# A kernel of four blocks on one core: the state-space stage's skip term as a diagonal product on TensorE, its input scaled by ScalarE, other orders of waits and steps

## The chip, the cores and the metric

One core of one Trainium2 chip runs the whole program. The metric is the time of one execution on the device in microseconds, as the median of several. The engines of the core are TensorE (PE in the profile, with its weight loads as PEld), VectorE (DVE), ScalarE (ACT), GpSimd (POOL) and SyncE (SP), which only issues transfers. Each works through its own list of instructions and waits on semaphores for the others.

## What is computed

The input is 16 sequences of 256 positions with 128 features, in float32. Four blocks follow each other, each fed with the layer norm of the running sum and added to it: a state-space block, a block of local attention and a gated product (two layers), a power-attention block, and the second one again. Only the first is touched. Cut to what matters:

```python
x    = resid * lax.rsqrt(jnp.mean(resid * resid, -1, keepdims=True) + EPS) * norm_w
skip = x @ skip_w.T
xe   = x @ in_w.T                       # 256 channels, then a causal convolution of 4 taps
xs   = silu(conv(xe) + conv_b)
delta = softplus(xs @ wd1.T @ wd2.T + wd2_b)
Bm, Cm = xs @ wb.T, xs @ wc.T           # 16 states
h    = exp(d_l * A) * h + (d_l * x_l) * b_l      # over the 256 positions
y_l  = sum over states of h * c_l
y    = y + xs * W_D                     # the skip term of the change
y    = (y * silu(skip)) @ out_w.T
return resid + y
```

## The kernel before

The 256 channels lie as two blocks (c) of 128 partitions, positions along the free axis. One sequence is a unit of work. Its 16 states are done in 8 groups g of 2, so a group is a tile of 128 x (2 states x 2 blocks x 256 positions) = 128 x 1024. The steps are named in four tables, and the number in a name is the group:

- TensorE: xT transposes the scaled input, xe is the input projection with the convolution folded in (8 matmuls), skip the gate's projection, u and z the two matmuls of delta, bc those of Bm and Cm, bB and bC broadcast one group's rows of Bm and Cm over the partitions, y adds up m_hc of a group into bank[1] by a product with the identity, out is the output projection.
- ScalarE: sq squares for the norm, xTe copies xT out with the weight of the norm, xs and gate are the SiLUs, abs, exp and ln belong to softplus, hi, mid and mid2 split Bm and Cm in bfloat16 parts, a is exp(delta A) of a group (4 instructions), c copies the broadcast Cm.
- VectorE: xr scales the input, ue copies u, r1 and lo are the rest of the split, delta ends softplus, bx is the product of a group into PSUM (L502), h its scan (L509), ys adds xs W_D to y (L514), yg multiplies with the gate (L519), x adds the output to the stream (L523).
- GpSimd: me and rr (the norm's root), dx, xx, and hc, the scan's result times c (two instructions, L547).

M_STAGES gives each step a stage 0, 1 or 2, and M_ORDER gives each engine's list. run_windows goes through an engine's list once per window k, and a step of stage n works on sequence k - n; so three sequences are under way at a time, and the engines' windows needn't coincide. The order is thus written out by hand. Every step signals one semaphore count; `m_before(s, i, step, g, back)` is the wait for the step that used the same buffer `back` groups ago. m_h and m_c have two buffers, m_hc four, and bank[1] holds y and then the output projection. Between the dependent engines the key lines are:

```python
pe.wait_ge(*dve_m.at(i, "lo"))                        # bB, bC
dve.wait_ge(*pe_m.at(i, f"bB{g}"))                    # bx
act.wait_ge(*m_before(dve_m, i, "h", g, 2))           # a
pool.wait_ge(*dve_m.at(i, f"h{g}"))                   # hc
```

## Time and profile before

| | |
|---|---|
| median of 3 runs | 3156.47 us (3153.13 to 3156.8) |
| profiled execution | 3154.61 us, span 3152.8 us |
| state-space stage | from about 31 to 597.6 us of the span |
| busy in the whole span | TensorE 86%, VectorE 78%, ScalarE 72%, GpSimd 43% |
| mean granted clock of TensorE | 0.954 |

The span goes from the first to the last instruction. Shares of busy time over the whole span mix stages with different limits; what the stage of the change is bound by is read in stretches within it. A timeline row gives the start, the busy time from the first to the last of the merged instructions, the engine, the line, the operation with its tiles, and in brackets the idle time before it with what ended it.

### The profile page before, as it was taken

The page shows a single profiled execution, that of the slowest core. Times are in us where ns is not written, and L with a number is a line of the kernel's source. Part 1 is how long each engine was busy: PE and PEld are TensorE (multiplying, and loading weights), DVE is VectorE, ACT ScalarE, POOL GpSimd, SP SyncE. Part 2 cuts the span into 40 slices and gives each one's busy share as a digit, 9 for nine tenths or more (in the row PEclk, how much of TensorE's full clock was granted, in tenths as well). Part 3 has the DMA queues.
Part 4 walks back from the last instruction along what each step waited for, and adds up shares of the span by engine and source line. Part 5 has one row for each costly group of instructions (what it writes and reads, how often), then busy time and mean ns, then how long its engine had stood idle before and what let it go on. Part 6 is the DMA issues. An engine that isn't in the chain of part 4 may idle for free. (4 is left out here: it accounts for less than half of the span.)

```text
span 3152.8 us, 55672 instructions
## 1 busy us (share of the span) xinstructions
PE 2699.7 (86%) x18784; PEld 1825.4 (58%) x18784; DVE 2472.1 (78%) x3831; ACT 2254.9 (72%) x5987; POOL 1352.2 (43%) x1073
## 2 busy tenths in 40 slices
PE   4888888579999999999669999995799999999996
PEld 2444444246666666666447777774566666666664
DVE  6999999767777777777468888887677777777773
ACT  4888888357767677677459999994577766777673
POOL 4666666535545455454310000001445544455452
PEclk9999999789999999999879999997899999999997
DMA  3000000000000000000000000000000000000000
GB/s 88 1 1 1 1 1 1 1 1 2 1 1 1 12 12 1 2 1 1 23 1 2 2 1 2 1 2 1 1 1 1 1 1 12 12 1 1 1 1 27
DMA packets 17237, 17.75 MB, mean 6 GB/s; under 512 B 3997, under 2 KB 14942, under 8 KB 16862
## 3 DMA queue, kind: packets, MB, share of 16 engines
q1 hardware_dynamic: 16958, 14.19, 1.5%
q8 instruction: 155, 2.54, 0.3%
q14 instruction: 124, 1.02, 0.1%
HBM read 12.09 MB, written 2.10 MB: 5 GB/s over the span
## 5 line engine op out<-in xcount | busy, mean ns | idle before, releaser
L906 POOL TENSOR_TENSOR f_p<-f_p,f_rs 128x512 f32<-128x512 f32 (+1 forms) x256 | 320.9, 1253 | 735.9 <-DVE f_rs L855 735.9
L751 ACT ACTIVATE f_p<-pair,f_nm 128x128 f32<-128x128 f32 (+1 forms) x1024 | 389.0, 392 | 192.5 <-DVE f_nm L844 191.7
L898 POOL TENSOR_TENSOR f_qb<-f_kn,f_tab 128x512 f32<-128x512 f32 x256 | 444.2, 1756 | 173.5 <-DVE f_kn L824 173.5
L547 POOL TENSOR_TENSOR m_hc<-m_h,m_c 128x512 f32<-128x512 f32 x256 | 328.5, 1304 | 170.9 <-DVE m_h L509 169.7
L509 DVE TENSOR_TENSOR_SCAN m_h<-m_a,pair 128x1024 f32<-128x1024 f32 x128 | 292.1, 2282 | 2.9
L705 PE MATMUL bank<-f_hnT,f_w 128*128 128x256 f32 (+1 forms) x768 | 214.0, 402 | 80.9 <-DVE f_u L881 77.7
L623 PE MATMUL pair<-f_wqkv,f_hT 128*128 128x512 f32 x512 | 256.9, 625 | 9.8 <-DVE f_kn L824 7.9
L814 DVE TENSOR_REDUCE f_ss<-f_sq 128x16 f32<-128x1024 f32 x128 | 155.2, 1212 | 139.5 <-ACT f_sq L722 139.5
L407 PE MATMUL bank<-m_hc,ident 128*128 128x512 f32 x512 | 258.5, 651 | 4.7 <-POOL m_hc L547 4.7
L666 PE MATMUL pair<-ident,f_p 128*128 128x128 f32 x1536 | 245.8, 283 | 16.6 <-POOL f_p L906 6.9
L1160 POOL TENSOR_TENSOR X<-X,p_y 128x256 f32<-128x256 f32 x16 | 11.7, 730 | 567.6 <-DVE p_y L1154 567.6
L830 DVE TENSOR_TENSOR f_qa<-f_kn,f_tab 128x1024 f32<-128x1024 f32 x128 | 240.3, 1877 | 0.2
L465 ACT ACTIVATE m_a<-m_delta,m_A 128x255 f32<-128x255 f32 x512 | 216.0, 495 | 25.1 <-DVE m_h L509 24.0
L680 PEld LDWEIGHTS pair<-f_pT,f_v 128*64 128x64 f32 x3072 | 149.7, 136 | 141.6 <-issue 139.0
L844 DVE TENSOR_REDUCE f_nm<-pair 128x4 f32<-128x512 f32 (+1 forms) x256 | 208.6, 815 | 12.2 <-PE pair L653 10.1
L837 DVE TENSOR_TENSOR f_qa<-f_qa,f_qb 128x1024 f32<-128x1024 f32 x128 | 185.1, 1446 | 41.0 <-POOL f_qb L898 41.0
L653 PE MATMUL pair<-f_kT,f_qT 64*128 64x128 f32 (+1 forms) x2048 | 212.9, 327 | 0.0
L751 ACT ACTIVATION_READ_ACCUMULATOR f_p<-pair,f_nm 128x1 f32 x1024 | 207.8, 203 | 0.0
L705 PEld LDWEIGHTS bank<-f_hnT,f_w 128*128 128x128 f32 (+1 forms) x768 | 123.7, 181 | 139.5 <-DVE f_u L881 106.4
L638 PE MATMUL bank<-ident,f_qa 128*128 128x128 f32 x1024 | 162.8, 282 | 48.2 <-DVE f_qa L837 40.7
L680 PE MATMUL pair<-f_pT,f_v 128*64 128x128 f32 (+1 forms) x3072 | 197.9, 264 | 5.8 <-DVE f_pT L849 4.0
L666 PEld LDWEIGHTS pair<-ident,f_p 128*128 128x128 f32 x1536 | 169.1, 142 | 57.0 <-POOL f_p L906 33.2
(181 smaller groups left out, 6563.5 us busy)
## 6 DMA issues: line engine op xcount, KB each, us to landing
f_wqkv<-in_f_wqkv SPq DMA_DIRECT2D x4, 768.0 KB, 4.0
X<-in_x SPq DMA_DIRECT2D x16, 128.0 KB, 2.6
out_x<-X SPq DMA_DIRECT2D x16, 128.0 KB, 2.0
f_w<-in_f_w SPq DMA_DIRECT2D x4, 341.0 KB, 3.4
f_wo<-in_f_wo SPq DMA_DIRECT2D x4, 256.0 KB, 2.7
sel<-in_sel SPq DMA_DIRECT2D x1, 768.0 KB
f_w<-in_f_w SPq DMA_DIRECT2D x4, 192.0 KB, 3.2
p_wqk<-in_p_wqk SPq DMA_DIRECT2D x1, 512.0 KB
```

The lines of the kernel that those rows point to most:

```text
L407: mm = nc.tensor.matmul(bank[1][:], ident[:], m_hc[:, g % 4, n].rearrange("p c l -> p (c l)"), start=g == 0 and n == 0, stop=g == NG - 1 a ...
L465: op = nc.scalar.activation(m_a[:, g % 2, n, c, 1:L], m_delta[:, b, c, 1:L], ACT.Exp, scale=m_A[:, c, g * GN + n:g * GN + n + 1])
L509: op = nc.vector.tensor_tensor_scan(m_h[:, g % 2].rearrange(flat), m_a[:, g % 2].rearrange(flat), pair[2][:], 0.0, ALU.mult, ALU.add)
L547: op = nc.gpsimd.tensor_tensor(m_hc[:, g % 4, n], m_h[:, g % 2, n], m_c[:, g % 2, n].unsqueeze(1).broadcast_to([P, EC, L]), ALU.mult)
L623: mm = nc.tensor.matmul(half(pair[0], n), f_hT[:, t * P:t * P + P], fw["wqkv"][:, n * 512:n * 512 + 512], start=True, stop=True)
L666: mm = nc.tensor.transpose(PT_PS[:, j * P:j * P + P], f_p[:, t, j, y * P:y * P + P], ident[:])
L680: mm = nc.tensor.matmul(OT_F[DH * e:DH * e + DH, c, q0:q1], f_v[:, b, y, h, :], w, start=y == 1 or t == 0, stop=y == 0, skip_group_check=True)
L705: mm = nc.tensor.matmul(bank[1][0:HR[c], n * L:n * L + L], fw["w1"][:, x * HID + c * P:x * HID + c * P + HR[c]], f_hnT[:], start=True, sto ...
L751: op = nc.scalar.activation(f_p[:, t, j, k0:k1], SC[:, j, k0:k1], ACT.Exp, bias=f_nm[:, t, j:j + 1], accum_out=f_sm[:, t, j:j + 1])
L830: op = nc.vector.tensor_tensor(f_qa[:, t].rearrange("p (x h) d -> p x h d", x=2), f_kn[:, t].rearrange("p (x h) d -> p x h d", x=2), f_tab ...
L898: op = nc.gpsimd.tensor_tensor(f_qb[:, t, :, o].rearrange("p (x h) d -> p x h d", x=2), f_kn[:, t, :, 32 - 32 * e:64 - 32 * e].rearrange(" ...
L906: op = nc.gpsimd.tensor_tensor(f_p[:, t, :, k0:k1], f_p[:, t, :, k0:k1], f_rs[:, t, :].unsqueeze(2).broadcast_to([P, 4, k1 - k0]), ALU.mult)
```

## The change

The skip term leaves VectorE: the tile m_skip holds, for each block, the identity times W_D, made once before the stage, and after the last y step two matmuls of 256 columns add m_skip times m_xs into the same PSUM bank. ys and its tile m_y are gone, and yg reads the bank itself. The scaling xr goes to ScalarE, as a copy with a scale for each partition; the constant factor (the root of 128) moves into m_nw, the norm's weight used in xTe. The waits of y, xTe, c, bx, h and hc stand in another order, the one for the producer last. xs now waits for yg of two sequences ago, as ys is gone. M_STAGES and M_ORDER are new for all four engines (their core is shown).

```diff
 M_ORDER = {
-    "dve": "bx5 h5 r1 bx6 delta h6 lo bx7 xr h7 bx0 h0 bx1 ys h1 yg bx2 h2 x bx3 h3 ue bx4 h4",
-    "pe": "bC7 y4 y5 bB0 bC0 xT bB1 bC1 y6 y7 xe bB2 bC2 out skip bB3 bC3 u bC4 bB4 y0 y1 bB5 z bB6 bC5 bc bC6 y2 y3 "
-        "bB7",
-    "act": "a0 xTe c0 a1 sq c1 a2 xs c2 a3 c3 a4 gate a5 c4 abs c5 exp hi a6 ln mid2 c6 c7 mid a7",
-    "pool": "hc0 hc1 hc2 me hc3 rr hc4 hc5 dx hc6 xx hc7"}
+    "dve": "bx1 h1 bx2 yg h2 bx3 h3 ue bx4 x h4 bx5 h5 r1 bx6 delta h6 lo bx7 h7 bx0 h0",
+    "pe": "bB7 bB0 y4 bB1 bC0 y5 y6 bC1 y7 bB2 xT bC2 bB3 xe bC3 skip bB4 u bB5 out bc bC4 z bC5 y0 bB6 y1 bC6 y2 y3 "
+        "bC7",
+    "act": "xTe sq c2 a3 xs c3 gate a4 c4 a5 abs c5 exp hi ln a6 mid2 a7 c6 mid a0 c7 a1 c0 xr a2 c1",
+    "pool": "dx hc6 xx hc7 me rr hc0 hc1 hc2 hc3 hc4 hc5"}
...
-        m_y = m_sb("m_y", [P, EC, L])
+        m_skip = m_sb("m_skip", [P, EC, P])
+        m_nw = m_sb("m_nw", [P, 1])
...
-                pe.wait_ge(*dve_m.at(i, "xr"))
+                pe.wait_ge(*act_m.at(i, "xr"))
...
             elif k == "y":
-                pe.wait_ge(*pool_m.at(i, f"hc{g}"))
                 if g == 0:
                     pe.wait_ge(*dve_m.at(i - 1, "x"))
+                pe.wait_ge(*pool_m.at(i, f"hc{g}"))
                 for n in range(GN):
                     mm = nc.tensor.matmul(bank[1][:], ident[:], m_hc[:, g % 4, n].rearrange("p c l -> p (c l)"),
-                                          start=g == 0 and n == 0, stop=g == NG - 1 and n == GN - 1)
+                                          start=g == 0 and n == 0, stop=False, skip_group_check=True)
+                if g == NG - 1:
+                    for c in range(EC):
+                        mm = nc.tensor.matmul(m_y_ps[:, c, :], m_skip[:, c, :], m_xs[:, b, c, :], start=False,
+                                              stop=c == EC - 1, skip_group_check=True)
...
+            elif s == "xr":
+                act.wait_ge(*pe_m.at(i - 1, "xT"))
+                act.wait_ge(*pool_m.at(i, "rr"))
+                for t in range(T):
+                    op = nc.scalar.activation(m_xr[:, t, :], tiles(seq(Z, z_at))[:, t, :], ACT.Copy, scale=m_rr[:, t:t + 1])
             elif s == "xTe":
+                act.wait_ge(const_set, 17)
+                act.wait_ge(*pe_m.at(i - 1, "skip"))
                 act.wait_ge(*pe_m.at(i, "xT"))
-                act.wait_ge(*pe_m.at(i - 1, "skip"))
-                op = nc.scalar.activation(m_xT[:, CONV - 1:], m_xT_ps, ACT.Copy, scale=mw["norm_w"][:])
+                op = nc.scalar.activation(m_xT[:, CONV - 1:], m_xT_ps, ACT.Copy, scale=m_nw[:])
...
             elif s == "xs":
                 act.wait_ge(*pe_m.at(i, "xe"))
-                act.wait_ge(*dve_m.at(i - 2, "ys"))
+                act.wait_ge(*dve_m.at(i - 2, "yg"))
                 for c in range(EC):
...
             elif k == "c":
+                act.wait_ge(*m_before(pool_m, i, "hc", g, 2))
                 act.wait_ge(*pe_m.at(i, f"bC{g}"))
-                act.wait_ge(*m_before(pool_m, i, "hc", g, 2))
...
-            if s == "xr":
-                dve.wait_ge(*pool_m.at(i, "rr"))
-                dve.wait_ge(*pe_m.at(i - 1, "xT"))
-                for t in range(T):
-                    op = nc.vector.tensor_scalar(m_xr[:, t, :], tiles(seq(Z, z_at))[:, t, :], m_rr[:, t:t + 1],
-                                                 float(D) ** 0.5, ALU.mult, ALU.mult)
-            elif s == "ue":
...
             elif k == "bx":
+                dve.wait_ge(*pool_m.at(i, "dx"))
                 dve.wait_ge(*pe_m.at(i, f"bB{g}"))
-                dve.wait_ge(*pool_m.at(i, "dx"))
                 dve.wait_ge(*m_before(dve_m, i, "h", g, 1))
...
             elif k == "h":
+                dve.wait_ge(*m_before(pool_m, i, "hc", g, 2))
+                dve.wait_ge(*act_m.at(i, f"a{g}"))
                 dve.wait_ge(*dve_m.at(i, f"bx{g}"))
-                dve.wait_ge(*act_m.at(i, f"a{g}"))
-                dve.wait_ge(*m_before(pool_m, i, "hc", g, 2))
...
-            elif s == "ys":
+            elif s == "yg":
+                dve.wait_ge(*pe_m.at(i - 1, "out"))
                 dve.wait_ge(*pe_m.at(i, f"y{M_LAST}"))
-                for c in range(EC):
-                    op = nc.vector.scalar_tensor_tensor(out=m_y[:, c, :], in0=m_xs[:, b, c, :], scalar=mw["W_D"][:, c:c + 1],
-                                                        in1=m_y_ps[:, c, :], op0=ALU.mult, op1=ALU.add)
-            elif s == "yg":
-                dve.wait_ge(*dve_m.at(i, "ys"))
-                dve.wait_ge(*pe_m.at(i - 1, "out"))
-                op = nc.vector.tensor_tensor(m_yg[:], m_y[:], m_gate[:, b], ALU.mult)
+                op = nc.vector.tensor_tensor(m_yg[:], m_y_ps, m_gate[:, b], ALU.mult)
...
             elif k == "hc":
+                pool.wait_ge(*m_before(pe_m, i, "y", g, 4))
+                pool.wait_ge(*act_m.at(i, f"c{g}"))
                 pool.wait_ge(*dve_m.at(i, f"h{g}"))
-                pool.wait_ge(*act_m.at(i, f"c{g}"))
-                pool.wait_ge(*m_before(pe_m, i, "y", g, 4))
...
+            nc.vector.tensor_scalar(m_nw[:], mw["norm_w"][:], float(D) ** 0.5, None, ALU.mult).then_inc(const_set, 1)
+            for c in range(EC):
+                op = nc.vector.tensor_scalar(m_skip[:, c, :], ident[:], mw["W_D"][:, c:c + 1], None, ALU.mult)
+            op.then_inc(const_set, 1)
```

What stands in a row on VectorE, before, from a product with ys behind it to the scan after ue (pair<- is the product bx, m_h the scan h):

```order
L502 TENSOR_TENSOR pair<-m_dx,pair 128x1024
L514 SCALAR_TENSOR_TENSOR m_y<-m_xs,m_W_D,bank 128x256 x2
L509 SCALAR_TENSOR_TENSOR m_h<-m_a,pair 128x1024
L519 TENSOR_TENSOR m_yg<-m_y,m_gate 128x512
L502 TENSOR_TENSOR pair<-m_dx,pair 128x1024
L509 SCALAR_TENSOR_TENSOR m_h<-m_a,pair 128x1024
L523 TENSOR_TENSOR X<-m_xx,bank 128x256
L502 TENSOR_TENSOR pair<-m_dx,pair 128x1024
L509 SCALAR_TENSOR_TENSOR m_h<-m_a,pair 128x1024
L484 COPY m_u<-bank 64x256
L502 TENSOR_TENSOR pair<-m_dx,pair 128x1024
L509 SCALAR_TENSOR_TENSOR m_h<-m_a,pair 128x1024
```

ys, yg, x and ue follow each other at one group's distance. VectorE at the same place after the change (lines are those of the new kernel: L506 the product, L513 the scan):

```order
L506 TENSOR_TENSOR pair<-m_dx,pair 128x1024
L518 TENSOR_TENSOR m_yg<-bank,m_gate 128x512
L513 SCALAR_TENSOR_TENSOR m_h<-m_a,pair 128x1024
L506 TENSOR_TENSOR pair<-m_dx,pair 128x1024
L513 SCALAR_TENSOR_TENSOR m_h<-m_a,pair 128x1024
L488 COPY m_u<-bank 64x256
L506 TENSOR_TENSOR pair<-m_dx,pair 128x1024
L522 TENSOR_TENSOR X<-m_xx,bank 128x256
L513 SCALAR_TENSOR_TENSOR m_h<-m_a,pair 128x1024
```

ys is gone, and yg and x now stand between a product and its scan; ue stands before x. r1, delta and lo keep their places; xr is gone from behind the product bx7.

ScalarE before, from xs (L437) over the exponentials a (L465) and the copies c (L470) to the gate (L431):

```order
L437 ACT_TABLE_LOAD
L437 ACTIVATE m_xs<-pair,m_conv_b 128x256 x2
L470 ACTIVATE m_c<-pair 128x512
L465 ACT_TABLE_LOAD
L465 ACTIVATE m_a<-m_delta,m_A 128x255 x4
L470 ACTIVATE m_c<-pair 128x512
L465 ACTIVATE m_a<-m_delta,m_A 128x255 x4
L431 ACT_TABLE_LOAD
L431 ACTIVATE m_gate<-pair 128x512
L432 ACT_TABLE_LOAD
L465 ACTIVATE m_a<-m_delta,m_A 128x255 x4
L470 ACTIVATE m_c<-pair 128x512
```

ScalarE after, from the scaling xr (L432) to the exponentials behind the gate (L441):

```order
L432 ACTIVATE m_xr<-Z,m_rr 128x128 x2
L475 ACTIVATE m_a<-m_delta,m_A 128x255 x4
L480 ACTIVATE m_c<-pair 128x512
L437 ACTIVATE m_xT<-bank,m_nw 128x256
L426 ACTIVATE m_sq,m_ss<-Z 128x128 x2
L480 ACTIVATE m_c<-pair 128x512
L475 ACTIVATE m_a<-m_delta,m_A 128x255 x4
L447 ACT_TABLE_LOAD
L447 ACTIVATE m_xs<-pair,m_conv_b 128x256 x2
L480 ACTIVATE m_c<-pair 128x512
L441 ACTIVATE m_gate<-pair 128x512
L442 ACT_TABLE_LOAD
```

Between xs and gate only one copy is left, and two of the four table loads of a sequence are gone; xr stands before the exponentials a2 of the same window.

TensorE before, from the transpose (L370) past y6 and y7 (the four of L407) to the output projection (L413):

```order
L370 MATMUL bank<-ident,m_xr 128x128 x2
L400 MATMUL pair<-m_bc,sel 128x256 x4
L407 MATMUL bank<-m_hc,ident 128x512 x4
L377 MATMUL pair<-m_xT,m_inc 128x256 x8
L400 MATMUL pair<-m_bc,sel 128x256 x4
L413 MATMUL bank<-m_out_w,m_yg 128x128 x4
```

TensorE after, from y5 and y6 over y7 and the diagonal product (L411) to the output projection (L417):

```order
L407 MATMUL bank<-m_hc,ident 128x512 x4
L400 MATMUL pair<-m_bc,sel 128x256 x2
L407 MATMUL bank<-m_hc,ident 128x512 x2
L411 MATMUL bank<-m_xs,m_skip 128x256 x2
L400 MATMUL pair<-m_bc,sel 128x256 x2
L370 MATMUL bank<-ident,m_xr 128x128 x2
L400 MATMUL pair<-m_bc,sel 128x256 x4
L377 MATMUL pair<-m_xT,m_inc 128x256 x8
L400 MATMUL pair<-m_bc,sel 128x256 x2
L382 MATMUL pair<-m_xT,m_skip_w 128x256 x2
L400 MATMUL pair<-m_bc,sel 128x256 x2
L417 MATMUL bank<-m_out_w,m_yg 128x128 x4
```

y4 to y7 and the diagonal product stand before the transpose now, and a broadcast (bC2) stands between the transpose and the convolution xe.

## Rows read from the trace of the kernel before

**Rows 1.** Stretch, its us; PE, PEld, DVE, ACT, POOL busy (counts); clock, DMA, GB/s.

```profile
188.00:256.00 68.00, 57.80 (x213) 31.04 (x212) 65.87 (x53) 56.03 (x116) 46.38 (x41) 0.93 0.00 1
```

**Rows 2.** Timeline, VectorE, from r1 to xr in one round.

```profile
140.93 0.42 DVE L488 TENSOR_TENSOR m_r<-bank,m_bc 32x256 f32<-32x256 f32 x1
141.38 1.23 DVE L502 TENSOR_TENSOR pair<-m_dx,pair 128x1024 f32<-128x1024 f32 x1
142.64 0.69 DVE L496 SCALAR_TENSOR_TENSOR m_delta<-pair,m_t 128x512 f32<-128x512 f32 x1
143.25 2.28 DVE L509 TENSOR_TENSOR_SCAN m_h<-m_a,pair 128x1024 f32<-128x1024 f32 x1
145.56 0.41 DVE L492 TENSOR_TENSOR m_bc<-m_r,m_mid 32x256 bf16<-32x256 f32 x1
146.00 1.23 DVE L502 TENSOR_TENSOR pair<-m_dx,pair 128x1024 f32<-128x1024 f32 x1
147.14 1.96 DVE L479 TENSOR_SCALAR m_xr<-Z,m_rr 128x128 f32<-128x128 f32 x2
```

**Rows 3.** Timeline, VectorE, the next round: ys, yg and x, then lo.

```profile
156.31 0.87 DVE L514 SCALAR_TENSOR_TENSOR m_y<-m_xs,m_W_D,bank 128x256 f32<-128x256 f32 x2
157.10 2.28 DVE L509 TENSOR_TENSOR_SCAN m_h<-m_a,pair 128x1024 f32<-128x1024 f32 x1
159.29 0.66 DVE L519 TENSOR_TENSOR m_yg<-m_y,m_gate 128x512 f32<-128x512 f32 x1
159.98 1.23 DVE L502 TENSOR_TENSOR pair<-m_dx,pair 128x1024 f32<-128x1024 f32 x1
161.25 2.29 DVE L509 TENSOR_TENSOR_SCAN m_h<-m_a,pair 128x1024 f32<-128x1024 f32 x1
163.45 0.40 DVE L523 TENSOR_TENSOR X<-m_xx,bank 128x256 f32<-128x256 f32 x1
163.76 1.22 DVE L502 TENSOR_TENSOR pair<-m_dx,pair 128x1024 f32<-128x1024 f32 x1
...
180.04 1.41 DVE L492 TENSOR_TENSOR m_bc<-m_r,m_mid 32x256 bf16<-32x256 f32 x1 [0.21 <-ACT m_mid L448]
```

**Rows 4.** Timeline, VectorE, the stage's first product and its last two scans.

```profile
50.10 1.22 DVE L502 TENSOR_TENSOR pair<-m_dx,pair 128x1024 f32<-128x1024 f32 x1
...
583.76 2.29 DVE L509 TENSOR_TENSOR_SCAN m_h<-m_a,pair 128x1024 f32<-128x1024 f32 x1
...
587.44 2.29 DVE L509 TENSOR_TENSOR_SCAN m_h<-m_a,pair 128x1024 f32<-128x1024 f32 x1
```

**Rows 5.** Timeline, GpSimd, the product hc behind the scan of 143.25.

```profile
145.61 2.73 POOL L547 TENSOR_TENSOR m_hc<-m_h,m_c 128x512 f32<-128x512 f32 x2 [0.90 <-DVE m_h L509]
```

**Rows 6.** One microsecond, columns as in rows 1: the clock is third from the end.

```profile
187.00:188.00 1.00, 1.00 (x3) 0.34 (x1) 0.96 (x2) 1.00 (x6) 1.00 (x2) 0.50 0.00 0
```

**Rows 7.** Timeline, TensorE: convolution, broadcasts, projection; two y steps, and two at half clock.

```profile
156.10 3.62 PE L377 MATMUL pair<-m_xT,m_inc 128*128 128x256 f32 x16
159.56 0.60 PE L400 MATMUL pair<-m_bc,sel 96*128 96x256 bf16 x4
...
161.01 1.03 PE L382 MATMUL pair<-m_xT,m_skip_w 128*128 128x256 f32 x4
...
165.16 3.60 PE L407 MATMUL bank<-m_hc,ident 128*128 128x512 f32 x8
...
185.40 5.29 PE L407 MATMUL bank<-m_hc,ident 128*128 128x512 f32 x8
```

**Rows 8.** Timeline, ScalarE, from xs over a copy and a table load to exponentials.

```profile
159.76 0.84 ACT L437 ACTIVATE m_xs<-pair,m_conv_b 128x256 f32<-128x256 f32 x2 [1.22 <-PE pair L377]
160.49 0.60 ACT L470 ACTIVATE m_c<-pair 128x512 f32<-128x512 f32 x1
161.10 1.28 ACT L465 ACT_TABLE_LOAD   x1
162.40 1.70 ACT L465 ACTIVATE m_a<-m_delta,m_A 128x255 f32<-128x255 f32 x4
```

More of the change, by code:

```diff
@@ L474, in m_dve @@
             k, g = s.rstrip("0123456789"), int("0" + s[len(s.rstrip("0123456789")):])
-            if s == "xr":
-                dve.wait_ge(*pool_m.at(i, "rr"))
-                dve.wait_ge(*pe_m.at(i - 1, "xT"))
-                for t in range(T):
-                    op = nc.vector.tensor_scalar(m_xr[:, t, :], tiles(seq(Z, z_at))[:, t, :], m_rr[:, t:t + 1],
-                                                 float(D) ** 0.5, ALU.mult, ALU.mult)
-            elif s == "ue":
+            if s == "ue":
                 dve.wait_ge(*pe_m.at(i, "u"))
@@ L529, in m_pool @@
                 pool.wait_ge(*act_m.at(i, "sq"))
-                pool.wait_ge(*dve_m.at(i - 1, "xr"))
+                pool.wait_ge(*act_m.at(i - 1, "xr"))
                 op = nc.gpsimd.tensor_tensor(m_rr[:], m_ss[:], eps_sum[:], ALU.add)
```

9 rows, old and new, of the table M_STAGES are left out of this document.

## The prediction

> **What bounds the kernel now.** Only the state-space stage is changed, so I first ask where it lies and who sets its pace. The busy time by stretch shows a steady piece of it: in 68 us VectorE is busy 65.87 us, TensorE 57.80, ScalarE 56.03, GpSimd 46.38, at a mean granted clock of 0.93 [rows 1]. VectorE is the one that is never late for anything but itself; the reader should see in its timeline that its rows stand shoulder to shoulder, with idle marked only at two small steps [rows 2, 3]. At the end of the stage, where nothing else stands between the scans, two scans start 583.76 and 587.44: 3.68 us for one group of states (product 1.26, scan 2.42) [rows 4]. The first product starts at 50.10 and the last scan ends at 587.44 + 2.29 = 589.73 [rows 4]: 539.6 us, of which 128 groups x 3.68 = 471.0. The other **68.6 us** are the small VectorE steps between the groups and its waits, 4.6 us for each of the 15 rounds that have them. That is what the change can win.
>
> **The change, part by part, on VectorE.** I price a small step by start-to-start distances, against 1.26 (product to scan) and 2.42 (scan to product), since a scan and an independent step overlap a little.
>
> *What goes.* The skip product ys takes 157.10 - 156.31 = 0.79 [rows 3], net 0.7. The input scaling xr takes 1.96 us in this round [rows 2]; it varies, and all of it goes.
>
> *What stays.* ue, r1, delta, lo keep their neighbours. delta: 143.25 - 142.64 = 0.61. lo: scan 143.25 to product 146.00 is 2.75, so 0.33; r1: 0.45 to the next product in place of the 0.13 gap, 0.3 to 0.35 [rows 2]. ue is a copy of the size of x, which cost 163.76 - 161.25 = 2.51 against 2.42, so 0.1 [rows 3].
>
> *What moves.* yg stood between scan and product (0.69 to the next start, net 0.46) and now stands between product and scan, with one operand in PSUM. delta is the nearest row: same size, PSUM operand, same position, 0.61 [rows 2]; I take that (bounds 0.46 and 0.69). x moves from a place where it cost 0.1 to one between product and scan, where its 0.40 counts nearly whole: 0.3 [rows 3].
>
> *What may go.* In every other round lo waits 0.21 for ScalarE and then takes 1.41 instead of 0.41 [rows 3, 2], 1.2 us more. The reason that I read: at 145.56 lo began 0.05 before GpSimd's product of 145.61, which then took 2.73; at 180.04 it came late [rows 2, 3, 5]. In the new ScalarE order the step mid, which lo waited for, stands behind r1 by mid2 0.4, four exponentials 1.65, a copy 0.6, mid 0.4, so 3.1 us after r1's end, and lo comes 4.2 us after it. So lo should be on time always, at 0.33.
>
> New round: 0.61 (yg) + 0.3 (x) + 0.1 (ue) + 0.35 (r1) + 0.61 (delta) + 0.33 (lo) = 2.3 us, x 15 = 34.5. Against 68.6 this saves **34 us**. The period of a sequence becomes 8 x 3.68 + 2.3 = 31.7 us.
>
> **Does another engine now set the period?** I lay one round from the end of lo (time 0), all others in place.
>
> TensorE per sequence was 57.80 / 2 = 28.9 busy for 34 us, partly at half clock [rows 1, 6]. It gains the diagonal product: two matmuls of 256 columns, as the gate's projection, 1.03 less the 0.17 by which rows overlap, 0.86 [rows 7]. A y step is (3.60 - 0.17) / 2 = 1.7, the convolution 3.45, a broadcast step 0.2. From lo: bB0, y4, bB1, bC0, y5, y6, bC1, y7 and the diagonal end at 8.7, bB2 at 8.9. The product bx2 wants bB2 at 11.0, yg wants y7 at 12.2. bC2 waits for ScalarE's c1, which stands behind a2 and so behind scan h0: 7.25 + 1.65 + 0.6 = 9.5. xTe, then the convolution 10.1 to 13.6. ScalarE: sq, c2, a3 until 12.8; its table load for xs waits for yg, which ends at 12.95; load 1.28, xs 0.73: 15.0. Projection 16.0, bB4, u: 17.1. VectorE asks for u at 18.8. Slack 1.7.
>
> ScalarE next: c3 beside it, gate 0.6 at 16.75, load 1.28, a4 (four exponentials, 1.65) until 19.7; scan h4 asks for it at 20.6. Slack 0.9, **the tightest**. That it holds at all is due to one effect of the order: xs and gate now stand with only a copy between them, so two of the four table loads of a sequence go, 2 x 1.30 (161.10 to 162.40 [rows 8]); against them stand two scalings of 128 columns, 0.5 in all (between nothing and one xs piece, 0.4, each). ScalarE falls from 28.0 to about 26 us of 31.7.
>
> The next instruction follows a load after 0.02 us [rows 8]. The Trainium skill (ScalarE: Activation LUTs, What ACT_TABLE_LOAD costs) gives 1283 ns for the load and some 1380 ns of drain on top; the first agrees, the second this trace doesn't show. By the page both remaining loads would each be 1.4 us longer, a4 would be 1.8 late, and 27 of the 34 us would be lost: 3149 us. I give it a chance of 0.01, within the second rival's.
>
> **The clock.** After idle stretches TensorE runs at 0.50, its 1.2 GHz level [rows 6], where two y steps take 5.29 - 0.17 = 5.1 instead of 3.4 us [rows 7]: 1.7 lost each time. In the new round TensorE is without a gap from 0 to 28, then waits for c6 and for lo, some 3 us. So I expect one slow stretch a round at most, over y4 and y5. Then y7 ends at 10.4 and bB2 at 10.6, still before 11.0; the rest of the chain moves by 1.2, u to 18.3 (in time), a4 to 20.9: **0.35 late**. In half to all of the rounds: 15 x 0.2 = 3 us lost, with 0 and 5 as ends.
>
> **Fill and drain.** In the first window bC2, xTe and the convolution of sequence 2 now stand behind a2, so behind h0; the convolution starts near 56.5 instead of 52.5, a4 some 0.6 later than now. I count 0.6 lost (0 to 2). At the end the diagonal product 0.86 stands where ys with 0.87 stood [rows 3, 7]: nothing. Two new setup steps on VectorE lie beside the first squares on ScalarE: nothing.
>
> **Order of waits.** A scan starts 1.26 after a product that takes 1.23 [rows 2], and GpSimd's product 0.08 after the scan's end (143.25 + 2.28 to 145.61 [rows 2, 5]), all three waits included. A better order can give no more than 0.03 a scan: 0 to 4 us over 128. I take 0.
>
> Sum: 34 - 3 - 0.6 = **31 us**. The profiled execution spans 3152.8 us and took 3154.61; the median of the runs is 3156.47, 1.9 above. Forecast 3156.5 - 31 = **3125.5 us**.
>
> **Rivals.**
>
> *lo always meets GpSimd.* The contest at 145.6 was won by 0.05 us. If the new order of GpSimd's waits (scan last) starts it a little sooner, lo loses each time and costs 1.4, 1.0 to 1.1 more: 15 x 1.05 = 16 lost, **3141 us**. For it: the margin. Against: lo follows the scan on its own engine and needs no signal. The rule by which this goes is stated in the Trainium skill (SBUF — State Buffer, Who interferes with whom): a VectorE instruction with two SBUF inputs and a GpSimd one that reads SBUF exclude each other, and the first to start keeps the port to its end. Chance 0.12.
>
> *TensorE gives it back.* Two slow stretches between lo and u: u at 20.5, a4 1.7 later again, period 31.7 + 2.1 = 33.8, 15 x 2.1 = 31 lost, and nearly all of the gain with it: **3154 us**. For it: 1.5 slow stretches a sequence now. Against: fewer gaps in the new order. Chance 0.07.
>
> *Slower.* The same loop, lo to bB0 to y7 to the convolution to u to ue and back to lo, becomes the bound. It has 1.7 us of slack; today's period lies 2.4 above the new one. So it makes the kernel slower from a delay of 4.1 us, which is 8 us of half clock in the 17 of the chain. With 10 us: delay 5, u 3.3 late, 15 x 3.3 = 50 against 34 saved: **3172 us**. Chance 0.06.
>
> *More.* No slow stretch matters, waits give their 4, other stages shift in favour: 3113 to 3118. Chance 0.1.
>
> **How the numbers follow.** Forecast (3118 to 3133, the ends of clock, yg, fill): 0.65; more 0.1; lo 0.12; TensorE 0.07; slower 0.06. A range from 3114 to 3144 leaves out the last two and little else. A measurement tells about 0.2%, 6.3 us, from no change. Faster by more: 0.65 + 0.1 + 0.12 = 0.87; within: 0.07; slower: 0.06.
>
> **What would show it.** VectorE's scans of one place in the round 31.7 to 32.1 apart in every round, not 34.1; lo at 0.4 in all rounds; no rows of ys or xr on VectorE; yg 0.67 to 0.7. Last scan's end near 558 instead of 589.7. ScalarE with 30 table loads fewer. One slow stretch a round, and idle of h4 for a4 of some 0.3. The sum is wrong if VectorE shows idle before ue or bx2 for TensorE, if lo takes 1.4, or if the later stages change length by more than 2 us.

## The result, and the profile after

The changed kernel takes 3132.78 us (median of 4 runs, 3131.54 to 3133.08); the kernel before, on the same chip, 3155.26. The ratio is 0.9929, with a 95% interval of 0.9916 to 0.9943: 22.5 us less. The forecast was 31 less (3125.5), with a range of 3114 to 3144. The direction and the range held; a quarter of the expected gain did not come. Below, the stretch of the stage means the time from the first product bx on VectorE to the end of the last scan, and a distance is the time from the start of one step to the start of the next.

A steady piece of the stage, busy time of each engine with the granted clock third from the end, answer to [rows 1]:

```profile
100.00:168.00 68.00, 60.71 (x235) 33.12 (x234) 64.68 (x48) 55.13 (x125) 48.30 (x42) 0.97 0.00 1
```

Columns are PE, PEld, DVE, ACT, POOL. VectorE is still the engine nearest to full, but it is busy 64.68 of 68 where it was 65.87. So it idles more than before (3.3 us in place of 2.1), although I expected less waiting. Where it idles shows in its timeline (start, duration, line, operation), to be read against [rows 2, 3]:

```profile
116.42 1.23 DVE L506 TENSOR_TENSOR pair<-m_dx,pair 128x1024 f32<-128x1024 f32 x1
117.78 2.29 DVE L513 TENSOR_TENSOR_SCAN m_h<-m_a,pair 128x1024 f32<-128x1024 f32 x1
120.20 1.23 DVE L506 TENSOR_TENSOR pair<-m_dx,pair 128x1024 f32<-128x1024 f32 x1
...
123.99 1.23 DVE L506 TENSOR_TENSOR pair<-m_dx,pair 128x1024 f32<-128x1024 f32 x1
125.12 0.68 DVE L518 TENSOR_TENSOR m_yg<-bank,m_gate 128x512 f32<-128x512 f32 x1
125.72 2.28 DVE L513 TENSOR_TENSOR_SCAN m_h<-m_a,pair 128x1024 f32<-128x1024 f32 x1
...
131.70 0.39 DVE L488 COPY m_u<-bank 64x256 f32<-64x256 f32 x1
132.02 1.21 DVE L506 TENSOR_TENSOR pair<-m_dx,pair 128x1024 f32<-128x1024 f32 x1
133.15 0.41 DVE L522 TENSOR_TENSOR X<-m_xx,bank 128x256 f32<-128x256 f32 x1
133.90 2.29 DVE L513 TENSOR_TENSOR_SCAN m_h<-m_a,pair 128x1024 f32<-128x1024 f32 x1 [0.35 <-ACT m_a L475]
...
142.33 2.28 DVE L513 TENSOR_TENSOR_SCAN m_h<-m_a,pair 128x1024 f32<-128x1024 f32 x1
144.63 0.41 DVE L496 TENSOR_TENSOR m_bc<-m_r,m_mid 32x256 bf16<-32x256 f32 x1
145.08 1.23 DVE L506 TENSOR_TENSOR pair<-m_dx,pair 128x1024 f32<-128x1024 f32 x1
```

Three readings. lo (L496) takes 0.41 in all 15 rounds and never waits. From a product to the scan right behind it there are now **1.36 us** (116.42 to 117.78). Before it was 1.26 (159.98 to 161.25 in [rows 3]; the prediction names rows 2, which has no such pair). The product's own 1.23 has not changed, and no wait is marked. This stands at 83 places. And the scan h4 waits 0.35 for ScalarE's a4, here just the figure forecast, but it comes later than its place in 6 rounds of 15 only.

The ends of the stage, to be read against [rows 4]:

```profile
50.75 1.23 DVE L506 TENSOR_TENSOR pair<-m_dx,pair 128x1024 f32<-128x1024 f32 x1 [0.76 <-PE pair L400]
...
67.00 0.42 DVE L488 COPY m_u<-bank 64x256 f32<-64x256 f32 x1 [1.25 <-PE bank L388]
...
69.47 2.29 DVE L513 TENSOR_TENSOR_SCAN m_h<-m_a,pair 128x1024 f32<-128x1024 f32 x1 [0.92 <-ACT m_a L475]
...
562.99 1.23 DVE L506 TENSOR_TENSOR pair<-m_dx,pair 128x1024 f32<-128x1024 f32 x1 [0.89 <-PE pair L400]
564.35 2.29 DVE L513 TENSOR_TENSOR_SCAN m_h<-m_a,pair 128x1024 f32<-128x1024 f32 x1
```

The stage's stretch, first product to the end of the last scan, is 564.35 + 2.29 - 50.75 = **515.9 us** against 539.6; 539.6 less the 31 of the prediction is 508.6. (Its sum has a slip: 34 - 3 - 0.6 is 30.4 and not 31, which would be 509.2 here and a forecast of 3126.1.) It starts 0.65 later, its tail is 0.13 longer, and the rest of the program came out 1.26 longer in this execution, within the 2 us in which the prediction had allowed it to move: 23.7 - 0.65 - 0.13 - 1.26 = 21.7, the difference of the two spans (3152.8 and 3131.1).

The 515.9, taken apart by distances:

| part of the stretch | forecast | measured |
|---|---|---|
| 128 groups x 3.68 | 471.0 | 471.0 |
| small steps, 15 rounds | 34.5 | 31.1 (yg 0.48, x 0.20, ue 0.11, r1 0.35, delta 0.61, lo 0.33) |
| first window and last product | 0.6 | 2.9 (1.36 at ue, 0.77 at h4, 0.75 at the last product; the waits are in the rows above) |
| scan h4 waiting for a4 in later rounds | 3 | 1.8 (6 times) |
| product to scan, 0.10 more, x 83 | 0 | **8.3** |
| three of these scans 0.35 later still | 0 | 1.1 |
| sum | 509.1 | 516.2 |

The sum exceeds the stretch by 0.3; 0.13 of it is that the last scan counts 2.42 in a group and takes 2.29. Why three scans (the first at 218.36) start 0.35 later than the others is not shown; they are missing where the scan's waits have their old order (e_scan_wait_old below).

TensorE's clock, in rows of the same place (four accumulations each, behind the same broadcast) in two successive rounds:

```profile
112.67 0.39 PE L400 MATMUL pair<-m_bc,sel 96*128 96x256 bf16 x2 [1.14 <-DVE m_bc L496]
112.90 2.81 PE L407 MATMUL bank<-m_hc,ident 128*128 128x512 f32 x4
...
145.10 0.39 PE L400 MATMUL pair<-m_bc,sel 96*128 96x256 bf16 x2 [1.14 <-DVE m_bc L496]
145.33 1.88 PE L407 MATMUL bank<-m_hc,ident 128*128 128x512 f32 x4
...
122.12 1.03 PE L411 MATMUL bank<-m_xs,m_skip 128*128 128x256 f32 x4
122.98 0.38 PE L400 MATMUL pair<-m_bc,sel 96*128 96x256 bf16 x2
```

The half-speed stretch comes in one of these two rounds, not in each: the clock is 0.59 from 113 to 117 and 1.00 from 143 to 147. Over the stage the steps y4 to y6 start at half pace in 6 of the 15 rounds, and these are the 6 in which h4 comes late, some 20 us further on (133.90 above belongs to the slow stretch at 113). The diagonal product takes 122.98 - 122.12 = 0.86, as forecast.

### The profile page after: what moved, and what is told of

Same layout as the page of the kernel before. It is cut to its first block and busy times, and to the rows that moved or that the text cites. A ratio compares the mean times of both kernels' runs of the same rounds, so it can differ in the third digit from the quotient of the medians.

```text
span 3131.1 us, 55741 instructions
## 1 busy us (share of the span) xinstructions
PE 2695.3 (86%) x18848; PEld 1828.4 (58%) x18848; DVE 2436.5 (78%) x3770; ACT 2221.8 (71%) x5989; POOL 1346.0 (43%) x1073
## 5 line engine op out<-in xcount | busy, mean ns | idle before, releaser
L546 POOL TENSOR_TENSOR m_hc<-m_h,m_c 128x512 f32<-128x512 f32 x256 | 322.2, 1280 | 153.9 <-DVE m_h L513 116.4
L513 DVE TENSOR_TENSOR_SCAN m_h<-m_a,pair 128x1024 f32<-128x1024 f32 x128 | 292.3, 2284 | 14.2 <-ACT m_a L475 2.7
L407 PE MATMUL bank<-m_hc,ident 128*128 128x512 f32 x512 | 247.4, 617 | 1.3 <-POOL m_hc L546 1.3
```

Of the source, the lines that this page charges most:

```text
L407: mm = nc.tensor.matmul(bank[1][:], ident[:], m_hc[:, g % 4, n].rearrange("p c l -> p (c l)"), start=g == 0 and n == 0, stop=False, skip_g ...
L513: op = nc.vector.tensor_tensor_scan(m_h[:, g % 2].rearrange(flat), m_a[:, g % 2].rearrange(flat), pair[2][:], 0.0, ALU.mult, ALU.add)
L546: op = nc.gpsimd.tensor_tensor(m_hc[:, g % 4, n], m_h[:, g % 2, n], m_c[:, g % 2, n].unsqueeze(1).broadcast_to([P, EC, L]), ALU.mult)
```

## The experiments

Every kernel below was timed beside the kernel before on its own chip, so ratios are compared; the stretches come from the profiled execution of each.

The theory: the 0.10 are what it costs when the wait that is satisfied last sits in the separate instruction. The rival: the 0.10 come from somewhere else in the new order of work. The changed kernel with the scan's waits in the old order:

```
-                dve.wait_ge(*m_before(pool_m, i, "hc", g, 2))
-                dve.wait_ge(*act_m.at(i, f"a{g}"))
                 dve.wait_ge(*dve_m.at(i, f"bx{g}"))
+                dve.wait_ge(*act_m.at(i, f"a{g}"))
+                dve.wait_ge(*m_before(pool_m, i, "hc", g, 2))
```

> The changed kernel, with the scan's three waits alone back in their former order (its product bx first, then the exponentials, then GpSimd). Theory of the waits: in the changed kernel a scan starts 1.36 us after the start of its product, before it was 1.26, at 83 places, so 8.3 us of the missing gain; here the distance is 1.26 again and the time falls by about 8, to 3124.5 us. Rival (the 0.10 comes from something else that changed, such as the tables of steps or where the tiles lie): the distance stays at 1.36 and the time at 3132.8.

3121.31 us, ratio 0.9902 (0.9889 to 0.9916). Its timeline, at the same place as above:

```profile
115.00 1.23 DVE L506 TENSOR_TENSOR pair<-m_dx,pair 128x1024 f32<-128x1024 f32 x1
116.26 2.29 DVE L513 TENSOR_TENSOR_SCAN m_h<-m_a,pair 128x1024 f32<-128x1024 f32 x1
```

The distance is 1.26 again (but for one place in the first window), the stretch 508.5: the sum that I had predicted (508.6). The trace also shows where the 0.10 lies. These are the separate instructions of two scans, of the one at 117.78 in the changed kernel and then of the one at 116.26 here (number, duration in ns, start):

```profile
L511 DVEq EVENT_SEMAPHORE  x1: 49/49/49, 117.7 to 117.7; - x1
```

```profile
L511 DVEq EVENT_SEMAPHORE  x1: 50/50/50, 115.0 to 115.0; - x1
```

In the changed kernel it holds the wait for the product. By the trace it starts 0.04 after the product's end, takes 0.05, and the scan starts 0.04 after it: 0.13. In the old order it holds the two other waits, is through while the product still runs, and the scan starts 0.03 after the product. In the median of the 83 places the instruction starts 0.04 after the product's end in the one kernel and 1.19 before it in the other.

The reverse, the new order of the scan's waits put alone into the kernel before:

> The kernel before, with the scan's three waits alone in the new order (product last). Theory of the waits: the 84 distances from product to scan go from 1.26 to 1.36 and the kernel is 8.4 us slower, 3163.7 us. Rival (something else of the change lengthens the distance): 1.26 stays, 3155.3 us.

3155.29 us, ratio 1.001 (1.0001 to 1.0019). The distance becomes 1.36 at 84 places, 8.1 us in all, and yet the stretch grows by 2.4 only (542.1), where I had expected the kernel 8.4 slower. The waits of VectorE show where the rest went (total us, times, longest), of the kernel before and then of this one:

```profile
DVE m_delta L496 <- ACT m_t L458: 3.3, 7, 0.5
DVE m_bc L492 <- ACT m_mid L448: 1.8, 7, 0.6
```

```profile
DVE m_delta L496 <- ACT m_t L458: 0.2, 1, 0.2
```

In the old order VectorE waited at delta and lo for ScalarE, and lo then met GpSimd's product and took 1.41. A slower VectorE arrives when ScalarE is done: over the stage the distances from lo to its product fall from 13.3 to 7.8, those from a product to delta from 22.0 to 19.0; against that the distances from xr to its scan, long or short by turns before, sum to 25.2 in place of 19.1. The cost of a wait order is the same 0.10, but whether it counts depends on whether the engine has slack elsewhere. Here is a wait order bettered in both kernels, the product's wait for the scan before it written first (shown as the edit of the kernel before; in the changed kernel dx stands ahead of bB):

```
-                dve.wait_ge(*pe_m.at(i, f"bB{g}"))
-                dve.wait_ge(*pool_m.at(i, "dx"))
                 dve.wait_ge(*m_before(dve_m, i, "h", g, 1))
+                dve.wait_ge(*pe_m.at(i, f"bB{g}"))
+                dve.wait_ge(*pool_m.at(i, "dx"))
```

In the changed kernel, together with the scan's old order:

> The changed kernel with the scan's waits in their former order, and the product's wait for the scan ahead of it written first too (it stood last in both kernels). If a wait that is written first costs 0.10 us less where it is the one that comes last, the distance from scan to product goes from 2.42 to 2.32 at some 81 places and the time falls by 8 more than with the scan's waits alone, to 3116.5 us. Rival (only the scan form is sensitive): 2.42 stays, 3124.5 us.

3114.49 us, ratio 0.9879 (0.9864 to 0.9894), stretch 500.4: scan to product is 2.32 instead of 2.42, and the sum over 82 places falls from 199.0 to 190.6. The same edit alone in the kernel before:

> The kernel before with one wait moved: the product's wait for the scan ahead of it is written first instead of last. The distance from scan to product goes from 2.42 to 2.32 at 52 places. Theory of the waits, if VectorE alone counts: 5 us faster. Rival, after the run in which the old kernel's longer distances were partly made good by shorter waits of delta and lo: those waits grow in turn, and it is within 3 us of before.

3153.85 us, ratio 0.9997 (0.9987 to 1.0006): no change, as the rival had it. The 0.10 is there again (52 distances, 126.1 to 121.4), but the distances from product to delta grow from 22.0 to 23.0, lo's distance to its product is 1.43 or more in 8 of 15 rounds, the distances from product to ys grow from 17.7 to 20.5, and the stretch ends 1.1 longer.

All waits of scan, product, exponentials, c and GpSimd's hc with the last comer first, in the changed kernel:

> As the last, and the waits of GpSimd's hc, ScalarE's exponentials a and copies c with the one that usually comes last written first. GpSimd's hc starts 0.07 instead of 0.17 us after its scan, a 0.10 sooner than now. VectorE sets the pace, so beyond the rare rounds in which a scan waits for its exponentials there is nothing to win: 3114 to 3116.5 us. Rival (a loop through GpSimd and ScalarE is near the bound): 3 us or more below the last kernel. Another: hc so much sooner meets lo on the shared port in each round, lo takes 1.4 and 15 us are lost, 3130.

**3111.45 us**, ratio 0.987 (0.9857 to 0.9884), stretch 499.4. That is 3.0 us less than with scan and product alone, and 1.0 of it is in the stretch. This is the fastest kernel of the study, about 41 us under the kernel before and, by the two ratios, about 19 under the changed one. Its timeline at the same place:

```profile
114.64 1.23 DVE L506 TENSOR_TENSOR pair<-m_dx,pair 128x1024 f32<-128x1024 f32 x1
115.91 2.29 DVE L513 TENSOR_TENSOR_SCAN m_h<-m_a,pair 128x1024 f32<-128x1024 f32 x1
118.23 1.23 DVE L506 TENSOR_TENSOR pair<-m_dx,pair 128x1024 f32<-128x1024 f32 x1
```

**What do the new lists carry, and what the moved operations?** First the skip term back on VectorE, in the changed kernel (ys ahead of h2, yg behind it; without the diagonal product):

```
-    "dve": "bx1 h1 bx2 yg h2 ..."
+    "dve": "bx1 h1 bx2 ys h2 yg ..."
```

> The changed kernel with the skip term back on VectorE (ys between a product and its scan, yg behind the scan) and no diagonal product on TensorE; all else as changed. Theory (VectorE sets the pace, and what it does counts whole): ys adds 0.79 less the 0.2 by which it hides the distance of 1.36 (1.14 to ys, 0.79), so 0.57, and yg behind a scan costs 0.46 instead of 0.38: 0.65 a round, x 15 = 10 us slower than the changed kernel, ratio 0.996 to the kernel before. Rival (TensorE is near the bound, and the diagonal's 0.86 matters there): at most 5 us slower, with the waits of the scan h4 for its exponentials gone.

3135.72 us, ratio 0.9945 (0.993 to 0.996), which overlaps the interval of the change; the stretch says it more sharply: 522.5, 6.6 longer, where I had expected 10. By distances: ys 1.14 + 0.78 - 1.36 = 0.56 and yg 0.36 come in, yg's 0.38 at its new place goes (here all against 1.36): 0.54 x 15 = 8.1, of which 1.4 are given back because the scan behind x waits less.

Next the input scaling back on VectorE, but at a new place, ahead of bx1:

```
-    "dve": "bx1 h1 bx2 ..."     "act": "... c0 xr a2 c1"
+    "dve": "xr bx1 h1 bx2 ..."  "act": "... c0 a2 c1"
```

> The changed kernel with the input scaling xr back on VectorE (two instructions ahead of bx1, the factor stays in m_nw), gone from ScalarE. Theory (VectorE sets the pace): between the scan h0 and the product bx1 it costs about 0.3 to 0.5 where it runs before GpSimd's hc of the same scan, 1.3 to 1.5 where hc is first and holds the shared port: 15 x 0.4 = 6 us slower at least, up to 22. Rival (ScalarE is near the bound through the exponentials of h4, and its 0.6 us matter as much): no change or faster than 3132.8.

3129.99 us, ratio 0.9926 (0.991 to 0.9943): no difference to the changed kernel, and a stretch 0.8 longer. The 6 to 22 us of the theory did not come. VectorE and GpSimd around xr (L484):

```profile
214.31 2.29 DVE L514 TENSOR_TENSOR_SCAN m_h<-m_a,pair 128x1024 f32<-128x1024 f32 x1
216.51 0.46 DVE L484 TENSOR_SCALAR m_xr<-Z,m_rr 128x128 f32<-128x128 f32 x2
216.89 1.22 DVE L507 TENSOR_TENSOR pair<-m_dx,pair 128x1024 f32<-128x1024 f32 x1
```

```profile
216.77 2.56 POOL L547 TENSOR_TENSOR m_hc<-m_h,m_c 128x512 f32<-128x512 f32 x2 [0.35 <-PE bank L407]
```

Both pieces of xr have begun before GpSimd's product does, and cost 2.20 + 0.37 - 2.42 = 0.15 a round. In the kernel before, where xr stands between product and scan, the like sum is 1.14 + 1.87 - 1.26 = 1.75 in rounds like that of [rows 2], and 0.73 in the others. GpSimd starts 0.17 after the scan's end (216.60), where it was 0.08 in [rows 2, 5]: its own wait for the scan is written last in the change too. Does that 0.10 protect xr? The best order of waits with xr at this place tells:

> The version with every wait of the group's steps written with the last comer first, and xr on VectorE ahead of bx1. In the changed kernel xr on VectorE cost 0.15 us a round and freed 0.6 on ScalarE, with no difference in the time. Here the rounds are 1 us shorter and ScalarE nearer its limit: if the scan h4's waits for its exponentials cost more by now, up to 3 us faster than without, 3109 us; else the same, ratio 0.987.

3133.47 us, ratio 0.993 (0.9913 to 0.9947): some 20 us above what I expected, and some 20 above the same waits with xr on ScalarE.

```profile
215.16 2.29 DVE L514 TENSOR_TENSOR_SCAN m_h<-m_a,pair 128x1024 f32<-128x1024 f32 x1
217.41 1.50 DVE L484 TENSOR_SCALAR m_xr<-Z,m_rr 128x128 f32<-128x128 f32 x2
218.84 1.22 DVE L507 TENSOR_TENSOR pair<-m_dx,pair 128x1024 f32<-128x1024 f32 x1
```

```profile
217.53 2.54 POOL L547 TENSOR_TENSOR m_hc<-m_h,m_c 128x512 f32<-128x512 f32 x2
```

GpSimd now starts 0.08 after the scan's end, and the distance from xr to the product is 1.42 in all 15 rounds (0.37 before); 2.25 + 1.42 - 2.32 = 1.35 a round, 20 us of the 21.2 by which the stretch is longer (520.6). In 3 rounds lo comes 0.2 late as well and takes 1.41, some 3.5 us, most of which shorter waits elsewhere make good. xr does begin 0.12 ahead of GpSimd, but it consists of two instructions. Their durations (shortest, median, longest in ns) and starts, first in the run before and then in this one:

```profile
L484 DVE TENSOR_SCALAR m_xr<-Z,m_rr x2: 262/272/281, 216.5 to 216.7; 128x128 f32<-128x128 f32 x2
```

```profile
L484 DVE TENSOR_SCALAR m_xr<-Z,m_rr x2: 286/792/1299, 217.4 to 217.6; 128x128 f32<-128x128 f32 x2
```

It is the second piece that is held: here it starts 0.09 after GpSimd and takes 1.30, to 218.91, when GpSimd's first half has just ended (218.83); with the later GpSimd it started 0.08 ahead of it (216.69 and 216.77) and took 0.28. That is so in all 15 rounds of both runs. The Trainium skill (SBUF — State Buffer, Who interferes with whom) counts tensor_scalar among the instructions that can take the ports shared with GpSimd, and says that whoever issues first keeps them for the whole instruction; the rows agree, taken instruction by instruction.

Then the new lists alone: ys and xr both on VectorE, at the new places, no diagonal product, all waits but xTe's in the order of the kernel before:

> The new lists alone: skip term on VectorE (ys), scaling xr on VectorE (ahead of bx1), all waits in their former order. From the single undoings: the changed kernel 3132.8, + 3 for the skip term in the time (+ 6.6 in the stage), + 0.8 for xr, - 8.3 for the scan's waits: 3131 to 3132 us, ratio 0.9925, if the parts add up. So the lists would carry all of the change's gain, through lo (0.41 in every round), two table loads fewer and xr out of GpSimd's way. Rival (the parts need each other): 3145 us or more.

3146.11 us, ratio 0.9971 (0.9959 to 0.9983), over 14 us above what I expected; the rival, that the parts need each other, had named 3145 or more. VectorE has no wait of more than 0.2 left in a steady round, and it has the two long steps:

```profile
186.17 1.51 DVE L481 TENSOR_SCALAR m_xr<-Z,m_rr 128x128 f32<-128x128 f32 x2
187.60 1.22 DVE L504 TENSOR_TENSOR pair<-m_dx,pair 128x1024 f32<-128x1024 f32 x1
...
192.41 0.87 DVE L516 SCALAR_TENSOR_TENSOR m_y<-m_xs,m_W_D,bank 128x256 f32<-128x256 f32 x2
```

Its stretch is 529.9. Against the 508.5 of the change with the scan's old waits, 15 x (2.20 + 1.43 - 2.42) = 18 us are xr and 15 x 0.54 = 8 are ys and the yg that it moves; some 5 come back from waits of h4, ue and the last product that this kernel does not have. The 18 are the port again: GpSimd starts at 186.34, the second piece of xr 0.01 to 0.02 later, and so in all 15 rounds. So the lists are worth about 10 us of the stretch by themselves (539.6 to 529.9), and the two operations that leave VectorE 21 more, most of it at xr.

Last the diagonal product alone, in the kernel before with its old lists (ys dropped from VectorE's list, nothing else moved):

> The kernel before, with its lists and waits, in which only the skip term moves to TensorE (diagonal product behind y7, yg reads PSUM; the step ys is struck from VectorE's list). Theory (what VectorE does counts whole): 15 x 0.7 = 10.7 us faster than before, ratio 0.9966. Rival (in the old lists delta and lo already wait for ScalarE in every other round, and a round that gets shorter on VectorE only waits more): between nothing and 5 us faster, with lo at 1.4 us and delta waiting in more than half of the rounds.

3162.85 us, ratio 1.0024 (1.0014 to 1.0034): **slower**, although VectorE has 0.79 us less to do in each round. VectorE around yg, then TensorE:

```profile
159.43 2.29 DVE L513 TENSOR_TENSOR_SCAN m_h<-m_a,pair 128x1024 f32<-128x1024 f32 x1
161.64 0.67 DVE L518 TENSOR_TENSOR m_yg<-bank,m_gate 128x512 f32<-128x512 f32 x1
163.55 1.23 DVE L506 TENSOR_TENSOR pair<-m_dx,pair 128x1024 f32<-128x1024 f32 x1 [1.24 <-PE pair L400]
```

```profile
158.81 1.03 PE L411 MATMUL bank<-m_xs,m_skip 128*128 128x256 f32 x4
159.67 3.62 PE L377 MATMUL pair<-m_xT,m_inc 128*128 128x256 f32 x16
163.13 0.60 PE L400 MATMUL pair<-m_bc,sel 96*128 96x256 bf16 x4
```

In the old list of TensorE the broadcast for bx2 stands behind y7 and the convolution. In [rows 7] it starts 159.56, and the product 159.98 [rows 3]: no slack. The diagonal puts 0.86 in front of it, while VectorE asks 0.79 sooner, and the product waits 1.24 here, 20.0 us over the stage. The 0.7 a round that ys gives back do not cover it, and the stretch grows from 539.6 to 549.0. In the new lists bB2 stands ahead of the convolution (122.98 in the rows of after), so nothing waits. The wait is measured; that the place of bB2 alone would cure it was not run. I had expected -10.7, or 0 to -5 by the rival: both missed. What the rival named did come (lo late in 10 of 15 rounds), but it is not what costs most.

**What do the two table loads carry that the new order of ScalarE saves?** The gate behind a4, which brings the table loads of a sequence from two back to four:

```
-    "act": "xTe sq c2 a3 xs c3 gate a4 c4 ..."
+    "act": "xTe sq c2 a3 xs c3 a4 gate c4 ..."
```

> The changed kernel with ScalarE's gate behind the exponentials a4 instead of ahead of them, so that the four table loads of a sequence are back (two more, 1.28 us each). Theory of my layout (ScalarE has slack but a narrow one): a4 now comes one load after c3 without waiting for the projection, so it is in time for its scan, while a5 and all behind it are 1.3 us later with some 1 to 2 us of slack: within 3 us of the changed kernel. Rival (the two loads saved are what makes room for the rest): the steps behind, c4, a5, abs to ln, make delta or the scans wait, 1 us a round, 15 us slower.

3145.93 us, ratio 0.9977 (0.9968 to 0.9986), stretch 533.6, 17.7 longer. I had put it within 3 us of the changed kernel; the rival, 15 us slower by delta or the scans, has the size but not the step that waits.

```profile
100.00:168.00 68.00, 57.60 (x232) 31.64 (x231) 64.47 (x47) 58.26 (x124) 46.05 (x41) 1.00 0.00 1
```

```profile
113.76 1.39 DVE L496 TENSOR_TENSOR m_bc<-m_r,m_mid 32x256 bf16<-32x256 f32 x1 [0.32 <-ACT m_mid L458]
115.18 1.23 DVE L506 TENSOR_TENSOR pair<-m_dx,pair 128x1024 f32<-128x1024 f32 x1
```

ScalarE is busy 58.3 instead of 55.1 and brings mid 0.3 late. lo misses its place and takes 1.39: the distance from scan over lo to product is 2.60 + 1.42 in place of 2.31 + 0.44, 1.27 more; lo is late in all 15 rounds, 18 us together. A delay of 0.3 costs four times its size, because GpSimd's product has begun by then. (The clock was 1.00 in these 68 us, and the kernel is the slower one.)

**Does a fuller TensorE keep its clock?** In the changed kernel the matmuls of bC7, the last thing before TensorE waits for lo, done three times over (each writes the same result):

```
-                for n in range(GN):
+                for n in list(range(GN)) * (3 if s == "bC7" else 1):
```

> The changed kernel with the two matmuls of the broadcast bC7 done three times over (same result), so that TensorE works 0.45 us more (0.9 at half clock) in the idle time ahead of lo. Theory of the clock (the scan h4 waits 0.35 for its exponentials in the rounds where y4 to y6 ran at 0.50 of the clock): fewer slow stretches, fewer waits of h4, 1 to 3 us faster. Rival (the waits of h4 have another cause): the slow stretches go and the waits stay, or neither changes, and the time stays at 3132.8.

3132.21 us, ratio 0.9931 (0.9917 to 0.9946); the clock of the steady piece stays 0.97, y4 to y6 start at half pace in 6 of 15 rounds again, though not in the same ones, and h4 waits as before. No effect, on the clock either, so it says nothing on what a full clock would bring. With 1.8 us of waits for a4 in all, there was little to win.

## Why the prediction was right, and where it was off

**Right in direction, and in the main in mechanism.** After the change VectorE sets the pace, ys and xr are gone from it, lo is on time in all 15 rounds, and no other engine becomes the bound; a round takes 32.0 us, up to 32.5 with a slow stretch, and the stage has 30 table loads fewer. yg was forecast at 0.61, from delta at the same position, and measured 0.48; x 0.3 and 0.20; ue, r1, delta and lo came as forecast. With the scan's old waits the change has a stretch of 508.5 against the 508.6 forecast, but that closeness is partly luck, by errors that offset each other: the steps were forecast 3.4 too high, and fill measured 3.3 there against 0.6.

**What was wrong about the kernel before.** The prediction said that VectorE "is never late for anything but itself", with idle marked at two small steps. These two are waits for ScalarE, at delta and at lo in 7 of 15 rounds each (3.3 and 1.8 us), and they tell more than their size: 5.7 of the 8.1 us added to it in e_before_scan_wait_new vanish in such waits and in the meetings with GpSimd. It was nearly full, but not alone in setting the pace.

**The step that failed: the order of waits, taken as 0.** I argued that a scan starts 0.03 after its product with all three waits in place, so a better order "can give no more than 0.03 a scan". That is true as a bound on a gain, and I read it as a bound on the effect. The edit could also lose, and the rows did have a price for that: the product starts 0.13 after the scan's end (2.42 against 2.29), and in it the wait for the scan is written last. A scan 0.10 later is just this. The runs show the step in both directions: 83 x 0.10 = 8.3 lost by the edit; when it is undone, 8.5 us back by the ratios of the two kernels and 7.4 by the stretch (h4 and ue wait some more there); and the same 0.10 gained at the products, a place for which the prediction had no term. It is as large as the whole shortfall of the forecast (31 to 22.5); the other errors nearly cancel.

**Fill, sized 0.6, measured 2.9.** I counted the first window by its convolution only. The wait of ue for u (1.25) stands behind it, and h4 waits behind that (0.92); the last product, which now has bB7 late in TensorE's list with no next sequence to cover it (0.89), I did not look at.

**Clock, sized 3, measured 1.8.** The slow stretch exists, and makes h4 wait up to 0.35 as worked out, but it comes in 6 of 15 rounds.

**Rival "lo always meets GpSimd".** Not in this kernel: GpSimd's new wait order starts it 0.10 *later*, not sooner as the rival feared. With that undone (3111.45 us) lo still takes 0.41 in all 15 rounds, since it starts 0.05 ahead of GpSimd. The mechanism is real, though: e_gate_behind_a4 turns it on in every round, by 0.3 of lateness, and v_all_first_xr in three.

**Rivals of TensorE.** VectorE waits for TensorE in the first window (1.25 at u) and from the last on (0.89 at a product, then the drain), and in no steady round. Without the new lists the diagonal does make VectorE wait for TensorE, but at bB2, a path that neither rival had.

**The parts.** The prediction took all of xr's cost as gone by moving it to ScalarE. In the changed kernel it would have cost 0.15 a round on VectorE at another place; with the waits put right, 1.35. So that all of it goes was right, but most of its price was the meeting with GpSimd, and not the work of xr.

**Open.** Not shown are why three scans start 0.35 later than the rest, why TensorE's slow stretch comes in the rounds in which it comes, and whether the place of bB2 alone would save the diagonal in the old lists.

## What to carry to other kernels

On the engine that sets the pace, write first the wait that is satisfied last; on an engine that has slack elsewhere, expect nothing from it. That an edit can gain little doesn't mean that it can't lose: price both sides by the nearest row. And before an operation moves to another engine, look which broadcast or transfer stands behind it there, since 0.86 us on an engine that is busy 57.80 of 68 us cost more here than 0.79 us on the one that is full.

## What the runs showed of the hardware that I had not expected

- A last-comer's wait in the separate semaphore instruction costs 0.10 us: on VectorE 0.13 instead of 0.03 after its own previous result, on GpSimd 0.17 instead of 0.08 after VectorE's. The instruction itself is 0.05 of it. It counts as no engine's busy time, and the timeline doesn't mark it as a wait.
- GpSimd's start 0.08 or 0.17 us after a scan decides whether two 128x128 scalings on VectorE right behind the scan cost 1.42 or 0.37 us, by the second of them alone (1.30 or 0.28).
- At the same place and behind the same wait of 1.14 us, TensorE has a clock of 1.00 in one round (its 2.4 GHz level) and 0.59 over four microseconds in another; half pace comes there in 6 rounds of 15, and three matmuls in place of each one ahead of the wait left it at 6. With better orders of waits it came less often (4 rounds in e_scan_wait_old, 2 in v_all_first).
